# Graph message passing on one core: picked-source sums get PSUM columns of their own, bases are read ahead of a wait, transposed x and the front of the result move in five pieces

## The chip, the cores and the metric

The kernel runs on one core of a Trainium2 chip. The metric is device time in microseconds (us) of one execution. The engines are TensorE (PE, matmuls; PEld, its weight loads), VectorE (DVE), ScalarE (ACT), GpSimd (POOL, which here issues the gathers) and SyncE (SP, which issues most other DMAs). Each engine works through its own instruction list in order and waits on semaphores.

## The reference

Nodes: 12,500 with 48 features. Edges: 400,000, sorted by destination, with 32 features each.

```python
h = jnp.maximum(_layernorm(x, axis=-1), 0.0)
x_i = h[dst]; x_j = h[src]
tmp = jnp.concatenate([x_i, x_j, edge_attr], axis=1)      # 400000 x 128
msg = jax.nn.relu(tmp @ W1 + b1) @ W2 + b2
out = x + jax.ops.segment_sum(msg, dst, num_segments=12500)
```

## The kernel before, in words

**Stage one** (up to about 80 us) normalises the nodes and makes two tables in DRAM, `a_table` (the h rows times the destination part of W1) and `b_table` (times the source part, with b1). It stores them in pieces; the last pieces set when the second stage may begin.

**Stage two** takes the edges in 782 groups of 512. A cycle is nine groups: eight **fetched** groups (696 in all), whose source rows POOL gathers from `b_table` with four indirect DMAs of 128 rows each (`gather_group`, L406), and one **picked** group (86 in all), whose source rows TensorE selects out of an SBUF table of h with one-hot matmuls, with no gather. There are 87 cycles; the last has no picked group of its own. Everything in a cycle is written as eight steps j = 0 to 7, and each engine has its own list of them. For step j, k = 8c + j:

- TensorE: `make_sums(k-3)` (L948, needs `r_ready`, the ReLU of group k-3), `make_z(k-1)` (L940, needs the transposed one-hot of DVE), `run_p(j)` (L964, ten matmuls of the picking), and at even j `fold` of the finished pair through W2 (L954, L955).
- DVE: `add_z(k-3)` (L715, PSUM result plus gathered rows), a share of the picked group's work (`key_hot` L739, `sum_picked` L761 to L769), the one-hots `make_hot` and `make_hot_t` (L695, L707) of group k, then at even j `copy_sums` (L719) and at odd j `add_out` (L730), which adds a folded pair into the result `out_sb` in SBUF at an address read from `base_i` (L729).
- ACT: `take_idx` (L487, gives POOL the indices of group k once the sums of group k-4 are done), `weigh_b2`, `rectify` (L503, the ReLU) and `pick` (L513, scales picked blocks).
- POOL: the gathers of group k, as soon as `idx_ready` allows it; there are four slots of gathered rows.
- SP: the edge, destination and `a_table` loads of group k, as soon as the product of group k-4 is done.

The picked group of cycle c-1 ends in cycle c. Its sums (`make_sums_p`) and its fold (`fold_p`) use the same PSUM columns as the pairs: `ps_sum[:, 0:WIN]`, `ps_out[:, 0:WIN]`, and the same SBUF tile `sums`. Therefore step 7 is written differently from the other odd steps (L1000 and L812 ff.): before anything of group k, DVE does `add_out(k-4)` and `copy_sums_p`, and TensorE does `make_sums_p`, `run_p` and `fold_p`, so that the columns are free in time:

```python
early = j == 7 and not first
if early:
    add_out(k - 4, it)
    copy_sums_p(c - 1, it)
```

**The result** `out_sb` lies in SBUF, transposed (48 x 12,500). It is first filled with transposed x by one DMA (L482) on ACT's queue, issued when both tables are stored, which is just when the second stage starts; the first `add_out` waits for it. At the end, the front 95% of it is stored by one DMA on SP's queue (L344), after SP has issued all loads and when the results that can still change it are in; the rest is stored at the very end (L368).

**The key row** of the first picked group is loaded (L300) after all stores of the tables have been issued.

Of the kernel before, what the change touches and what calls it, by code (L numbers as in the profile page):

```python
# [13 lines left out]
P = 128  # L14
# [13 lines left out]
def gnn(nc, x_main, x_last, x_t, src_t, src_p, dst_t, dst_n, edge_t, w1, b1, w2, b2, out_t):  # L28
# [26 lines left out]
    front = n_nodes * 95 // 100  # L55
    gen_cols, gen_k = 500, 5
# [6 lines left out]
    assert rounds * gen_cols * gen_k == n_nodes  # L63
# [8 lines left out]
    with ctx:  # L72
# [17 lines left out]
        sums = sb("sums", [P, 2 * WIN])  # L90
        idx = sb("idx", [P, SLOTS, TILES], I32)
# [77 lines left out]
        ps_out = ps[0:feat, 3, 0:2 * WIN]  # L169
        ps_cov = ps[0:1, 4, 0:1]  # L170
# [64 lines left out]
        def _(sp):  # L235
# [30 lines left out]

            for c in range(chunks):
# [28 lines left out]
            def load_key(c, it, first=False):  # L296
                n = c + it
                if not first:
                    sp.wait_ge(p_hot_ready, TILES * n)
                sp.dma_start(p_key, key_flat[:, ds(n * e_cols, e_cols)].partition_broadcast(P)).then_inc(p_key_in, 16)  # L300
# [23 lines left out]
            sp.wait_ge(key_stored, 16)  # L324
            sp.wait_ge(h_ready, chunks)
            load_key(0, 0, True)
# [11 lines left out]

            sp.wait_ge(settled_ready, 1)
            front_settled = sp.value_load(settled[0:1, 0:1], min_val=0, max_val=1)  # L340
            with sp.If(front_settled > 0):
                sp.wait_ge(out_added, fetched - late)
                sp.wait_ge(p_out_added, items - 1)
                sp.dma_start(out_t[:, 0:front], out_sb[:, 0:front]).then_inc(out_stored, 16)  # L344
            with sp.Else():
                sp.nop()
# [21 lines left out]
            sp.dma_start(out_t[:, front:n_nodes], out_sb[:, front:n_nodes]).then_inc(out_stored, 16)  # L368
            with sp.If(front_settled < 1):
                sp.dma_start(out_t[:, 0:front], out_sb[:, 0:front]).then_inc(out_stored, 16)  # L370
            with sp.Else():
                sp.nop()
            sp.wait_ge(out_stored, 32)
# [55 lines left out]
        def _(act):  # L429
# [52 lines left out]
            act.dma_start(out_sb, x_t).then_inc(xt_in, 16)  # L482
# [50 lines left out]
            def cycle(c, it, first=False, final=False):  # L533
                for j in range(PERIOD):
# [36 lines left out]
        def _(dve):  # L571
# [149 lines left out]
            def add_out(k, it, after_p=None):  # L721
                dve.wait_ge(folded, it * (PERIOD // 2) + k // 2 + 1)
                if after_p is not None:
                    dve.wait_ge(p_out_added, after_p + it + 1)
                for h in range(2):
                    s, g = it * PERIOD + k - 1 + h, group_of(k - 1 + h, it)
                    if k > 1 or h:
                        dve.wait_ge(out_added, s)
                    base = dve.value_load(base_i[0:1, ds(g, 1)], min_val=0, max_val=n_nodes - WIN)  # L729
                    nc.vector.tensor_tensor(out_sb[:, ds(base, WIN)], ps_out[:, h * WIN:(h + 1) * WIN],  # L730
                                            out_sb[:, ds(base, WIN)], ALU.add).then_inc(out_added, 1)
# [60 lines left out]
            def copy_sums_p(c, it):  # L792
                dve.wait_ge(p_summed, c + it + 1)
                nc.vector.tensor_copy(sums[:, 0:WIN], ps_sum[:, 0:WIN]).then_inc(p_copied, 1)

            def add_out_p(c, it, k):
                n, g = c + it, p_group(c, it)
                dve.wait_ge(p_folded, n + 1)
# [294 lines left out]
```

## Time and profile before

| what | value |
|---|---|
| median of three runs | 3669.01 us (3666.77, 3669.01, 3681.05) |
| profiled execution | 3678.76 us, span 3676.9 us, 1.9 us outside of the span |
| TensorE busy | 3480.5 us (95%), mean granted clock 0.948 of full |
| POOL busy | 2655.2 us (72%), in 2784 gathers |
| DVE busy | 2592.4 us (71%) |
| ACT busy | 1780.6 us (48%) |
| DMA traffic | 380.40 MB, mean 103 GB/s |

The span runs from the first to the last instruction. The busy time of an engine leaves out register, branch, semaphore and DMA-issuing instructions, so the share of POOL above leaves out the time between two gathers.

### The profile page before, as it was taken

To read this page: it belongs to the slowest core of one execution; us is meant where nothing else is said; L and a number is where in the kernel's file an instruction comes from. 1 tells how busy PE (TensorE), PEld (TensorE's weight loads), DVE (VectorE), ACT (ScalarE), POOL (GpSimd) and SP (SyncE) were. 2 spreads that over 40 slices of the span, in tenths; PEclk is the share of its full clock that TensorE was granted. 3 is DMA by queue.
4 is the path that set the end of the run, shared out by engine and by line. 5 is a ranking of instruction groups with operands and counts; after the bars stand their busy time and mean duration, and the time that the engine had idled before them with its cause. 6 is when DMAs were issued, how large, how long until landed. Compare 5 with 4: busy or idle time off the path is not lost.

```text
span 3676.9 us, 90266 instructions
## 1 busy us (share of the span) xinstructions
PE 3480.5 (95%) x22112; PEld 3043.2 (83%) x22112; DVE 2592.4 (71%) x6238; ACT 1780.6 (48%) x5902; POOL 2655.2 (72%) x2800
## 2 busy tenths in 40 slices
PE   7899999999999999999999999999999999999997
PEld 6788888888888888888888888888888888888887
DVE  6667676767777777767776777777776776777674
ACT  5444444444444445444544454444444444445443
POOL 1677777777777777777777777777777777777775
PEclk9899999999999999999999999999999999999997
DMA  8433333333333333333333333333333333333333
GB/s 270 105 98 100 103 97 96 100 104 96 98 97 106 95 98 98 102 97 99 99 100 98 97 101 103 98 98 98 102 99 98 98 103 98 95 99 104 96 98 94
DMA packets 268638, 380.40 MB, mean 103 GB/s; under 512 B 86052, under 2 KB 149333, under 8 KB 267878
## 3 DMA queue, kind: packets, MB, share of 16 engines
q0 software_dynamic: 89088, 182.63, 19.5%
q1 hardware_dynamic: 179462, 195.11, 17.9%
q10 hardware_dynamic: 64, 2.40, 0.5%
q8 instruction: 8, 0.13, 0.0%
q14 instruction: 16, 0.13, 0.0%
HBM read 362.77 MB, written 17.03 MB: 103 GB/s over the span
## 4 chain that ended last, share of the span: by engine, by line
PE 81%; DVE 6%; DVEq 5%; issue 4%; ACT 2%; DMA 1%; SPq 0%; POOL 0%; ACTq 0%; POOLq 0%
PE ps L964 39%; PE ps L940 17%; PE ps L948 16%; PE ps L954 3%; DVEq L729 3%; DVE p_hot L739 2%; PE ps L981 2%; DVE gath L715 2%; PE ps L955 2%; ACT gath L503 2%; DVEq L800 1%; PE ps L974 1%; PE ps L914 1%; DVE nodes L730 1%; DMA rhs<-a_table 1%
## 5 line engine op out<-in xcount | busy, mean ns | idle before, releaser
L406 POOL DMA_INDIRECT gath<-b_table,idx x2784 | 2651.1, 952 | 999.5 <-issue 900.2
L964 PE MATMUL ps<-h_tab,p_hot 128*128 128x480 f32 x6880 | 1793.6, 410 | 9.5 <-DVE p_hot L739 9.5
L964 PEld LDWEIGHTS ps<-h_tab,p_hot 128*128 128x128 f32 x6880 | 1332.2, 202 | 205.4 <-issue 9.6
L513 ACT ACTIVATE work<-ps,work 128x96 f32<-128x96 f32 x3440 | 869.9, 344 | 636.7 <-PE ps L964 597.7
L503 ACT ACTIVATE gath<-gath 128x512 f32<-128x512 f32 x696 | 439.7, 632 | 1110.2 <-DVE gath L715 1110.1
L948 PEld LDWEIGHTS ps<-onehot,gath 128*128 128x128 f32 x5568 | 711.1, 195 | 218.5 <-ACT gath L503 163.1
L948 PE MATMUL ps<-onehot,gath 128*128 128x48 f32 x5568 | 750.0, 279 | 146.3 <-ACT gath L503 146.3
L940 PE MATMUL ps<-rhs,lhs 96*128 96x128 f32 x5568 | 815.1, 291 | 16.3 <-DVE lhs L707 16.3
L940 PEld LDWEIGHTS ps<-rhs,lhs 96*128 96x128 f32 x5568 | 706.9, 199 | 17.0 <-DVE lhs L707 16.9
L730 DVE TENSOR_TENSOR nodes<-ps,nodes 48x48 f32 x696 | 139.4, 200 | 823.1 <-PE ps L955 486.8
L707 DVE TENSOR_SCALAR_CACHE_REDUCE lhs<-nodes 48x512 f32<-48x512 f32 x696 | 517.9, 744 | 50.1 <-DMA rhs<-a_table 19.7
L739 DVE TENSOR_TENSOR p_hot<-work,ps 128x1280 fp32r<-128x1280 f32 x344 | 508.1, 1477 | 8.2 <-DMA work<-key_row 7.4
L715 DVE TENSOR_TENSOR gath<-ps,gath 128x512 f32<-128x512 f32 x696 | 480.9, 691 | 15.6 <-DMA gath<-b_table,idx 7.3
L695 DVE TENSOR_TENSOR onehot<-ps,dst_rel 128x192 f32<-128x192 f32 x696 | 245.2, 352 | 2.7
L496 ACT ACTIVATE b_deg<-b_bc,deg 48x48 f32<-48x48 f32 x696 | 234.7, 337 | 16.8
L761 DVE TENSOR_TENSOR work<-work 128x480 f32<-128x480 f32 x344 | 223.5, 650 | 0.0
L487 ACT COPY idx<-src_sb 128x4 int32 (+1 forms) x692 | 137.4, 199 | 88.4 <-PE ps L948 64.5
L954 PEld LDWEIGHTS ps<-sums,w_sb 128*48 128x48 f32 x696 | 58.0, 123 | 122.1 <-issue 121.2
L763 DVE TENSOR_TENSOR work<-work 128x192 f32<-128x192 f32 x344 | 126.5, 368 | 11.8
L719 DVE COPY sums<-ps 128x96 f32<-128x96 f32 x348 | 88.0, 253 | 65.8 <-PE ps L948 61.8
L954 PE MATMUL ps<-sums,w_sb 128*48 128x96 f32 x696 | 129.1, 268 | 0.4 <-DVE sums L719 0.3
L955 PE MATMUL ps<-pair_ident,b_deg 112*48 112x96 f32 x696 | 115.7, 247 | 0.0
(88 smaller groups left out, 1416.8 us busy)
## 6 DMA issues: line engine op xcount, KB each, us to landing
nodes<-dst_row SPq DMA_DIRECT2D x782, 96.0 KB
lhs<-in_edge_t SPq DMA_DIRECT2D x696, 64.0 KB
gath<-b_table,idx POOLq DMA_INDIRECT x2784
work<-key_row SPq DMA_DIRECT2D x86, 256.0 KB
rhs<-a_table SPq DMA_DIRECT2D x696, 24.0 KB
work<-in_edge_t SPq DMA_DIRECT2D x172, 32.0 KB
b_table<-nodes SPq DMA_DIRECT2D x7, 512.0 KB, 3.3
a_table<-nodes SPq DMA_DIRECT2D x7, 512.0 KB, 5.2
```

Source lines behind the costliest of these rows:

```text
L406: pool.indirect_dma_start(gath[:, u, t, :], None, b_table, bass.IndirectOffsetOnAxis(ap=idx[:, u, t:t + 1], axis=0)).then_inc(gathered[u], 16)
L496: nc.scalar.activation(b2_deg[r:r + WIN, k // 2 % 2, :], b2_bc[0:WIN, :], ACT.Copy, scale=deg[:, u:u + 1]).then_inc(b2_ready, 1)
L503: nc.scalar.activation(z, z, ACT.Relu).then_inc(r_ready, 1)
L513: m = nc.scalar.activation(p_sel[:, t % 2, RUN_COLS * q + j, :], ps_run[:, r % 2, j * split:(j + 1) * split], ACT.Copy, scale=p_mask[:, RU ...
L695: nc.vector.tensor_tensor(onehot[:, u, :, :], iota_ps.unsqueeze(1).to_broadcast([P, TILES, WIN]), dst_rel[:, ds(g * TILES, TILES)].unsquee ...
L707: nc.vector.tensor_scalar(lhs[0:WIN, u, :], dst_bc[:, u, :], first_node[:, ds(g, 1)], None, ALU.is_equal, ALU.add, accum_out=deg[:, u:u + ...
L715: nc.vector.tensor_tensor(z, ps_z[:, k % 2, :], z, ALU.add).then_inc(z_added, 1)
L739: nc.vector.tensor_tensor(p_hot[:, t % 2, :, :], p_key[:, t * P:(t + 1) * P].unsqueeze(1).to_broadcast([P, BLOCKS, P]), key_iota_ps.unsque ...
L940: mm = nc.tensor.matmul(ps_z[:, k % 2, t * P:(t + 1) * P], lhs[:, u, t * P:(t + 1) * P], rhs[:, u, :], start=True, stop=True)
L948: mm = nc.tensor.matmul(ps_sum[:, k % 2 * WIN:(k % 2 + 1) * WIN], gath[:, u, t, :], onehot[:, u, t, :], start=(t == 0), stop=(t == TILES - 1))
L954: nc.tensor.matmul(ps_out, w2_sb[:], sums[:], start=True, stop=False)
L964: mm = nc.tensor.matmul(ps_run[:, r % 2, :].rearrange("p (j w) -> p j w", j=RUN_COLS), p_hot[:, t % 2, i, :], h_parts[:, first:first + BLO ...
```

## The change

1. The picked group's sums and its fold get columns of their own in the same two PSUM banks (`ps_sum_p`, `ps_out_p`, columns 96 to 144), and an SBUF tile `sums_p`.
2. With that, step 7 has the order of the other odd steps. TensorE does `make_sums_p` at the end of step 7 ahead of `run_p`, and `fold_p` at the end of the next cycle's step 0. DVE does `copy_sums_p` in the next cycle's step 0 and `add_out_p` in its step 1. In step 1 `add_out` waits for `fold_p` too, since it reads the same bank.
3. `add_out` reads both bases from `base_i` ahead of its wait for the fold; before, each was read behind the wait. `add_out_p` reads its base ahead of its wait too.
4. The key row of the first picked group is loaded in stage one, ahead of the last chunk's table stores.
5. Transposed x is loaded in five DMAs of 2500 columns, which ACT issues in step 3 of the first cycle, behind the ReLU of group 0.
6. The front of the result is stored in five DMAs of 2375 columns, which SP issues in steps 3 to 7 of the last cycle between its loads.

```diff
+        ps_sum_p = ps[:, 2, 2 * WIN:3 * WIN]
+        ps_out_p = ps[0:feat, 3, 2 * WIN:3 * WIN]
...
+                if c == 5:
+                    sp.wait_ge(key_stored, 16)
+                    sp.wait_ge(h_ready, chunks)
+                    load_key(0, 0, True)
...
+            def store_front(k):
+                part = slice(k * front_piece, (k + 1) * front_piece)
+                if k == 0:
+                    sp.wait_ge(settled_ready, 1)
+                    sp.wait_ge(out_added, fetched - late)
+                    sp.wait_ge(p_out_added, items - 1)
...
+                    if final and j >= 3:
+                        store_front(j - 3)
...
-            act.dma_start(out_sb, x_t).then_inc(xt_in, 16)
+
+            def load_x(k):
+                act.dma_start(out_sb[:, k * piece:(k + 1) * piece], x_t[:, k * piece:(k + 1) * piece]).then_inc(xt_in, 16)
...
+                    if first and k == 3:
+                        for x in range(pieces):
+                            load_x(x)
...
-            def add_out(k, it, after_p=None):
+            def add_out(k, it, after_p=None, beside_p=None):
+                bases = [dve.value_load(base_i[0:1, ds(group_of(k - 1 + h, it), 1)], min_val=0, max_val=n_nodes - WIN)
+                         for h in range(2)]
                 dve.wait_ge(folded, it * (PERIOD // 2) + k // 2 + 1)
+                if beside_p is not None:
+                    dve.wait_ge(p_folded, beside_p + it + 1)
...
-                    early = j == 7 and not first
-                    if early:
-                        add_out(k - 4, it)
-                        copy_sums_p(c - 1, it)
...
-                    if early:
-                        add_out_p(c - 1, it, k - 4)
...
+                        add_out(k - 4, it, c - 2 if j == 3 and c > 1 else None, c - 2 if j == 1 and c > 1 else None)
+                    if j == 1 and c > 1:
+                        add_out_p(c - 2, it, k - 4)
...
+                    if j == 0 and c > 1:
+                        copy_sums_p(c - 2, it)
...
-                    if j == 7 and not first:
-                        make_sums_p(c - 1, it)
-                        if not final:
-                            run_p(j, c, it)
-                        fold_p(c - 1, it)
...
+                    if j == 7 and not first:
+                        make_sums_p(c - 1, it)
+                    if not final:
                         run_p(j, c, it)
                     if j % 2 == 0 and k >= 4:
                         fold(k - 3, it)
+                    if j == 0 and c > 1:
+                        fold_p(c - 2, it)
```

How the lists move: on TensorE, step 7 of a cycle before (L948 is `make_sums`, L940 `make_z`, L964 `run_p`, L988 `make_sums_p`, L993 and L994 `fold_p`; line numbers of the kernel before).

```order
L988 MATMUL ps<-work 128x48 [waits p_r_ready]
L988 MATMUL ps<-work 128x48 x3
L961 REGISTER_ALU
L964 MATMUL ps<-h_tab,p_hot 128x480 [waits p_picked]
L964 MATMUL ps<-h_tab,p_hot 128x480 x9
L993 MATMUL ps<-sums,w_sb 48x48 [waits p_copied]
L994 MATMUL ps<-ident,p_b_deg 48x48
L948 MATMUL ps<-onehot,gath 128x48 [waits r_ready]
L948 MATMUL ps<-onehot,gath 128x48 x3
...
L940 MATMUL ps<-rhs,lhs 128x128 [waits hott_ready]
L940 MATMUL ps<-rhs,lhs 128x128 x3
```

The same step of the changed kernel (its lines stand 22 lines further down: L970 is `make_sums`, L962 `make_z`, L1010 `make_sums_p`, L986 `run_p`).

```order
L970 MATMUL ps<-onehot,gath 128x48 [waits r_ready]
L970 MATMUL ps<-onehot,gath 128x48 x3
L960 REGISTER_ALU
L962 MATMUL ps<-rhs,lhs 128x128 [waits hott_ready]
L962 MATMUL ps<-rhs,lhs 128x128 x3
L1010 MATMUL ps<-work 128x48 [waits p_r_ready]
L1010 MATMUL ps<-work 128x48 x3
L986 MATMUL ps<-h_tab,p_hot 128x480 [waits p_picked]
L986 MATMUL ps<-h_tab,p_hot 128x480 x9
```

The picked fold has left step 7, and the ten picking matmuls now come last in it. On DVE, step 7 of a cycle before, from the copy of the pair's sums of step 6 on (L729 and L730 are `add_out`, L794 `copy_sums_p`, L715 `add_z`, L739 `key_hot`).

```order
L719 COPY sums<-ps 128x96 [waits summed]
...
L729 REGISTER_ALU [waits out_added,folded]
L729 TENSOR_LOAD base_i
...
L730 TENSOR_TENSOR nodes<-ps,nodes 48x48
L729 REGISTER_ALU [waits out_added]
L729 TENSOR_LOAD base_i
...
L730 TENSOR_TENSOR nodes<-ps,nodes 48x48
L794 COPY sums<-ps 128x48 [waits p_summed]
...
L715 TENSOR_TENSOR gath<-ps,gath 128x512 [waits gathered0]
...
L739 TENSOR_TENSOR p_hot<-work,ps 128x1280 [waits p_run_done]
```

The same place of the changed kernel (L734 is `add_z`, L760 `key_hot`, L714 and L726 the one-hots, L741 and L751 `add_out`).

```order
L738 COPY sums<-ps 128x96 [waits summed]
...
L734 TENSOR_TENSOR gath<-ps,gath 128x512 [waits gathered0]
...
L760 TENSOR_TENSOR p_hot<-work,ps 128x1280 [waits p_run_done]
...
L714 TENSOR_TENSOR onehot<-ps,dst_rel 128x192
...
L726 TENSOR_SCALAR lhs,deg<-nodes 48x512
...
L741 TENSOR_LOAD base_i
...
L741 TENSOR_LOAD base_i
...
L751 ISA [waits out_added,folded]
L751 TENSOR_TENSOR nodes<-ps,nodes 48x48
L751 ISA [waits out_added]
L751 TENSOR_TENSOR nodes<-ps,nodes 48x48
```

The wait for the fold has moved from ahead of `add_z` to the end of the step, and both reads of the bases stand ahead of it.

## Rows read from the trace of the kernel before

**Rows 1.** The waits, longest first: engine, line, waited for, us, times, longest

```profile
DVE nodes L730 <- PE ps L955: 486.8, 168, 4.2
PE ps L948 <- ACT gath L503: 146.3, 88, 8.1
POOL gath L406 <- ACT idx L487: 99.3, 155, 16.1
```

**Rows 2.** Timeline of TensorE, one step 7: start, us, line, tile, [idle <-releaser]

```profile
2016.65 2.45 PE L964 MATMUL ps<-h_tab,p_hot 128*128 128x480 f32 x10
...
2020.39 1.12 PE L940 MATMUL ps<-rhs,lhs 96*128 96x128 f32 x8
2023.12 1.09 PE L948 MATMUL ps<-onehot,gath 128*128 128x48 f32 x8 [1.60 <-ACT gath L503]
2024.04 1.23 PE L940 MATMUL ps<-rhs,lhs 96*128 96x128 f32 x8
2024.93 3.99 PE L964 MATMUL ps<-h_tab,p_hot 128*128 128x480 f32 x10
```

**Rows 3.** The same line a cycle later, and two neighbours in another place

```profile
2063.93 1.09 PE L948 MATMUL ps<-onehot,gath 128*128 128x48 f32 x8 [1.60 <-ACT gath L503]
...
3043.20 1.09 PE L948 MATMUL ps<-onehot,gath 128*128 128x48 f32 x8 [1.60 <-ACT gath L503]
...
3082.45 1.42 PE L948 MATMUL ps<-onehot,gath 128*128 128x48 f32 x8 [1.60 <-ACT gath L503]
```

**Rows 4.** Timeline of DVE ahead of that step's add_z

```profile
2016.65 0.20 DVE L730 TENSOR_TENSOR nodes<-ps,nodes 48x48 f32 x1 [4.17 <-PE ps L955]
2017.68 0.20 DVE L730 TENSOR_TENSOR nodes<-ps,nodes 48x48 f32 x1 [0.83 <-DVE nodes L730]
```

**Rows 5.** Timeline of POOL: first waits, a steady stretch, a pause, the last gather

```profile
83.67 1.10 POOL L406 DMA_INDIRECT gath<-b_table,idx  x1 [78.83 <-issue]
...
119.64 0.95 POOL L406 DMA_INDIRECT gath<-b_table,idx  x1 [16.12 <-ACT idx L487]
...
134.65 0.95 POOL L406 DMA_INDIRECT gath<-b_table,idx  x1 [0.30 <-issue]
...
508.60 0.94 POOL L406 DMA_INDIRECT gath<-b_table,idx  x1 [2.04 <-issue]
...
2021.67 0.95 POOL L406 DMA_INDIRECT gath<-b_table,idx  x1 [0.89 <-ACT idx L487]
...
3654.58 0.94 POOL L406 DMA_INDIRECT gath<-b_table,idx  x1 [0.30 <-issue]
```

**Rows 6.** Busy time by stretch: us, busy us of each engine, clock, DMA share, GB/s

```profile
2000.00:2040.00 40.00, 38.40 (x249) 33.41 (x248) 28.78 (x70) 20.05 (x67) 29.96 (x32) 0.96 0.36 101
```

**Rows 7.** The start of stage two on all engines, and the DMA issues

```profile
85.08 0.40 ACTq L482 DMA_DIRECT2D nodes<-in_x_t  x1
85.87 4.04 SPq L294 DMA_DIRECT2D rhs<-a_table  x4
...
107.93 0.74 DVE L707 TENSOR_SCALAR_CACHE_REDUCE lhs<-nodes 48x512 f32<-48x512 f32 x1 [19.68 <-DMA rhs<-a_table]
...
nodes<-in_x_t ACTq DMA_DIRECT2D x1, 2343.8 KB, 22.1
```

**Rows 8.** DMA queues from 89 to 101 us: packets, MB, share (q10 ACT, q0 POOL)

```profile
q10 hardware_dynamic: 32, 1.60, 102.2%
q0 software_dynamic: 17, 0.07, 4.3%
```

**Rows 9.** The end: SP, then DVE, and the store's issue row

```profile
3638.98 0.33 SPq L344 DMA_DIRECT2D out_t<-nodes  x1
...
3656.61 0.69 DVE L715 TENSOR_TENSOR gath<-ps,gath 128x512 f32<-128x512 f32 x1 [7.33 <-DMA gath<-b_table,idx]
...
3667.85 0.67 DVE L715 TENSOR_TENSOR gath<-ps,gath 128x512 f32<-128x512 f32 x1
...
out_t<-nodes SPq DMA_DIRECT2D x1, 2226.6 KB, 17.4
```

More of the change, by code:

```diff
@@ L55, in gnn @@
     front = n_nodes * 95 // 100
+    pieces = 5
+    piece, front_piece = n_nodes // pieces, front // pieces
     gen_cols, gen_k = 500, 5
@@ L62, in gnn @@
     assert PERIOD == 2 * SLOTS
-    assert rounds * gen_cols * gen_k == n_nodes
+    assert rounds * gen_cols * gen_k == n_nodes and piece * pieces == n_nodes and front_piece * pieces == front
     a_table = nc.dram_tensor("a_table", [padded, hidden], F32).ap()
@@ L294, in load_a @@
                 sp.dma_start(rhs[0:WIN, u, :], a_table[ds(base, WIN), :]).then_inc(loaded[u], 16)
[L296 to L300, printed above, removed]
+            def store_front(k):
[4 more added lines that the diff above has]
+                    sp.wait_ge(p_out_added, items - 1)
+                front_settled = sp.value_load(settled[0:1, 0:1], min_val=0, max_val=1)
+                with sp.If(front_settled > 0):
+                    sp.dma_start(out_t[:, part], out_sb[:, part]).then_inc(out_stored, 16)
+                with sp.Else():
+                    sp.nop()
             def load_p(c, it, first=False):
@@ L337, in _ @@
             cycle(cycles - 1, 0, final=True, more=False)
[L339 to L346, printed above, removed]
             sp.wait_ge(flag_ready, 1)
@@ L368, in _ @@
             sp.dma_start(out_t[:, front:n_nodes], out_sb[:, front:n_nodes]).then_inc(out_stored, 16)
+            front_settled = sp.value_load(settled[0:1, 0:1], min_val=0, max_val=1)
             with sp.If(front_settled < 1):
-                sp.dma_start(out_t[:, 0:front], out_sb[:, 0:front]).then_inc(out_stored, 16)
+                for k in range(pieces):
+                    part = slice(k * front_piece, (k + 1) * front_piece)
+                    sp.dma_start(out_t[:, part], out_sb[:, part]).then_inc(out_stored, 16)
             with sp.Else():
                 sp.nop()
-            sp.wait_ge(out_stored, 32)
+            sp.wait_ge(out_stored, 16 * (pieces + 1))
         @block.gpsimd
@@ L725, in add_out @@
                 for h in range(2):
-                    s, g = it * PERIOD + k - 1 + h, group_of(k - 1 + h, it)
                     if k > 1 or h:
[L728 to L731, printed above, removed]
+                        dve.wait_ge(out_added, it * PERIOD + k - 1 + h)
+                    nc.vector.tensor_tensor(out_sb[:, ds(bases[h], WIN)], ps_out[:, h * WIN:(h + 1) * WIN],
+                                            out_sb[:, ds(bases[h], WIN)], ALU.add).then_inc(out_added, 1)
             def key_hot(t, c, it):
@@ L854, in _ @@
                 if k % 2:
-                    add_out(k - 4, 0, items - 1)
+                    add_out(k - 4, 0, None, items - 1)
+                    add_out_p(items - 1, 0, k - 4)
                 else:
                     copy_sums(k - 3, 0)
-            add_out(fetched - 1, 0)
+                if k == fetched:
+                    copy_sums_p(items - 1, 0)
+            add_out(fetched - 1, 0, items - 1)
             outside = dve.value_load(flag[0:1, 0:1], min_val=0, max_val=n_edges)
@@ L1012, in cycle @@
                         make_z_p(c - 1, it)
-                    if not final and (j != 7 or first):
+                    if j == 7 and not first:
+                        make_sums_p(c - 1, it)
+                    if not final:
                         run_p(j, c, it)
@@ L1022, in _ @@
             cycle(0, 0, first=True)
-            with pe.Fori(0, cycles - 2) as it:
-                cycle(1, it)
+            cycle(1, 0)
+            with pe.Fori(0, cycles - 3) as it:
+                cycle(2, it)
             cycle(cycles - 1, 0, final=True)
@@ L1031, in _ @@
                     fold(k - 3, 0)
+                if k == fetched:
+                    fold_p(items - 1, 0)
             outside = pe.value_load(flag[0:1, 0:1], min_val=0, max_val=n_edges)
```

26 lines of the change are left out of this document (14 added, 12 removed).

## The prediction

> **What bounds the kernel now.** I read the waits first. TensorE waits for one thing that counts, the ReLU of the fetched group: 88 times, 146.3 us in all [rows 1]. The timeline of TensorE shows where: once a cycle, in step 7, the second `make_sums` is late [rows 2]. It starts 2.73 us after the `make_z` ahead of it (2020.39 to 2023.12), where the next such pair, which waits for nothing, is 0.89 apart (2024.04 to 2024.93): a stall of 1.84 us. Behind the stall the ten picking matmuls take 3.99 us instead of 2.45: the clock has been taken to its lower level (1.2 GHz) for a while, and that costs 1.54 us more. The same line comes back after 40.81 us (2023.12 to 2063.93) [rows 2, 3], which is the cycle's length. The reader is to check this on the cycle that begins at 3043.20: it took 39.25 us [rows 3], 1.56 less, which is what a cycle costs when the clock does not fall. So TensorE's own work is 40.81 - 1.84 - 1.54 = 37.43 us a cycle.
>
> The cause of the stall is on DVE: `add_out` waits 4.17 us for the fold of step 6, and the `add_z` of step 7 is queued behind it [rows 4].
>
> Then I ask who is next. POOL is 72% busy by its row, but that row leaves out the time between gathers. In the timeline a gather takes 0.95 us and 0.30 passes before the next [rows 5], so 32 gathers of a cycle need 40.0 us at the least. POOL is nearly as full as TensorE. From the gather at 119.64 to the last at 3654.58 there are 2767 steps in 3534.94 us, 86.5 cycles. The waits for ACT's indices are 99.3 us, 155 times [rows 1]; less the first, 16.1, and less 154 usual gaps of 0.30, true waiting is 37.0 us. All the rest is POOL's own, pauses such as the 2.04 us at 508.60 too [rows 5]: 3534.94 - 37.0 = 3497.9 us, **40.44 us a cycle**. TensorE holds the kernel at 40.81, and POOL is 0.37 behind it. DVE is busy 28.8 of 40 us, ACT 20.1 [rows 6].
>
> The start and the end have chains of their own. DVE waits 19.68 us for `a_table` rows that SP issued from 85.87 on, since ACT had issued transposed x at 85.08, which takes 22.1 us to land [rows 7]. From 89 to 101 us that load moves 1.60 MB and fills the engines (102%), while all gathers together get 0.07 MB through [rows 8]. At the end the store of the front does the same: issued at 3638.98, 17.4 us, and `add_z` waits until 3656.61 for gathered rows [rows 9].
>
> **The change, part by part.**
>
> *Step 7.* The stall of 1.84 and, with it, the slow matmuls of 1.54 go: `add_z` is no longer queued behind a wait for the fold, and what `make_sums_p` and `fold_p` do is moved, not added. TensorE's share would be 3.38 x 86.5 = 292 us. But POOL allows only 40.81 - 40.44, that is the 37.0 us of index waits. So the term is **37 us**. Its bounds: at the top POOL also loses its pauses, 3534.94 - 2767 x 1.25 = 76 us; at the bottom a third of the waits turn out to be pauses that are put down to ACT, 25 us.
>
> *The moved pieces.* `fold_p` now lengthens step 0 of TensorE and `copy_sums_p` and `add_out_p` lengthen steps 0 and 1 of DVE, each by well under a microsecond. They lie beside POOL's 40.44: TensorE has 3.0 us a cycle to spare. Without that cover they would cost nothing either, for their number is the same as before. What is late next is the gathered row: TensorE will wait for the ReLU before most steps, some 0.4 us each, as each group's gathers take 40.44 / 8 = 5.05 us and an average step 4.68. The indices of a group are due four groups ahead, so POOL should not feel it.
>
> *The bases.* Between the two adds lie 0.83 us, nearly all of it the read of a base [rows 4]. Read ahead, it hides in the wait for the fold. DVE wins about 0.6 us on each of 348 pairs, and none of it is on the path in the loop: zero. At the very end it is on the path once, 0.8 us, counted below.
>
> *The key row.* Its DVE wait at the start ended long before the 19.68 us one, and rows of a table land last in either order. Zero, or a microsecond either way, as it stands ahead of the last table stores.
>
> *Transposed x.* The `a_table` rows, issued at 85.87, should land at about 88.3 instead of 107.9, and the steps 0 to 3 run about 19.6 us earlier. ACT then issues x near 97. Its bytes still need 15 to 22 us of the same DMA engines, so it lands between 113 and 120 and holds up the gathers of groups 2 to 5 meanwhile. POOL issues these without a pause, as their indices are ready: the 16.12 us gap [rows 5] closes. It next has to stop at group 7, whose indices need the sums of group 3, whose rows land after x: 120, then some 4 us for add, ReLU, sums and indices, so 124.5, against 134.65 before [rows 5]. The term is **10 us**. Bounds: 83.67 + 28 x 1.25 = 118.7, no stop at all, 16 us; and 4 us if the loads of SP that share the queues make x land at 126.
>
> On this the Trainium skill's "DMA: Bandwidth & Descriptors", section "Queues, rings and completion order", says that each DMA engine takes turns between its queues, a packet at a time. The trace agrees, 1.60 MB of long rows against 0.07 MB of gathers [rows 8]. By that rule five shorter pieces let five times as many small packets pass, and the term would be nearer its upper bound, 16 us. I stay with 10: a group's 512 gathered rows are 32 for each of 16 engines, and the 5 x 48 long rows of x give each engine only 15 turns to pass them.
>
> *The front's store.* SP is three to four groups ahead when it issues in steps 3 to 7, so the last piece is out no later than the single store was (3638.98), and needs 17.4 / 5 = 3.5 us: landed by 3645, with POOL gathering until 3655.5. The last rows then land some 2.5 us after POOL ends, and from the last `add_z` at 3667.85 to the end are 9.05 us [rows 9], less 0.8 for the base. The end after POOL's last gather is 10.8 us in place of 3676.9 - 3655.5 = 21.4: **10.6 us**. Bounds 5 (the groups queue up on a TensorE at the lower clock) and 12.
>
> *Sum.* 37 + 10 + 10.6 = 57.6 us. The profiled execution took 3678.8, so its successor would take 3621. It stands 9.8 us above the median of the runs, 3669.0, so the forecast for the median is **3612 us**. With the bounds: 104 us to 34 us, 3565 to 3635.
>
> **The rivals.**
>
> *The whole stall comes back.* If POOL could follow, 292 + 21 us would go: 3356 us. Against it: 1.25 us a gather, 16 times in a row without any wait. 3%.
>
> *POOL's pauses shrink too.* They are not bound to anything that I can name; if they go, 3669 - 76 - 21 = 3572 us. 12%.
>
> *Another wait takes its place.* If the cycle stays at 40.81, for instance since a DVE step of 5.2 us (step 1 has both adds and the picked one) pushes its successors, only start and end are won: 3648 us. For it: four slots couple all engines. Against: DVE's busy share. 12%.
>
> *The clock falls more often: slower.* TensorE now idles once a cycle for 1.84 us and its clock falls once. Afterwards it idles a little before most steps. Each fall costs 1.54 us. POOL's 40.44 covers (40.44 - 37.43) / 1.54 = 2.0 falls a cycle. Start and end give 20.6 us, and 18.3 more makes 0.5%, so the kernel is slower from a cycle of 40.81 + 38.9 / 86.5 = 41.26 on, 2.5 falls a cycle. At three, the cycle is 42.05 and the time 3669 + 107 - 21 = 3755 us. Against it: a TensorE that is behind POOL has no idle time, and then its clock has no reason to fall. 5%.
>
> The Trainium skill's "TensorE: Matmul & The Clock Gate", section "A second HAM failure mode: psum-queue depth-cycling", says that frequent very short idle times between groups of matmuls can make the clock go down and up again. The trace has no such pattern, only one long idle time a cycle; by that rule this rival would be the likeliest, with 3755 us or more.
>
> *Start or end go wrong by over 20 us* (x starves the gathers for longer than before): about 3650 us with the 37 kept. 2%.
>
> **How the numbers follow.** My forecast has 66%, and its own range is 3580 to 3635 us. To leave out no more than 2 in 10, I reach from POOL's pauses (3572) to the case of an unchanged cycle (3648). Half a per cent, 18 us, is about what a measurement tells from no change: 3651 and up is no gain. Faster: 66 + 12 + 3, and 7 of the 12 for the unchanged cycle, 88%. The same: 5 and 2, 7%. Slower: 5%.
>
> **What would show it.** In the changed profile: POOL's waits for ACT's indices nearly gone behind the start; gathers 1.25 us apart through steps 7 and 0; a cycle near 40.4 us; TensorE waiting for ReLU several times a cycle, shortly, with few or no picking groups of 3.9 us; DVE waiting for gathered rows (7.3 us before, once) in hundreds of places; DVE's first one-hot near 88 us and a long wait there for x or for rows near 110 to 120; the end about 11 us behind the last gather. The forecast is wrong if the cycle is not set by POOL: then look for picking groups of 3.9 us (clock), or for index waits that stay (another ring of waits).

## The result

The changed kernel takes 3608.55 us, median of four runs (3607.37 to 3610.1), against 3667.91 for the kernel before (3666.77 to 3681.05): a ratio of 0.983, 95% interval 0.9807 to 0.9853, or 59.4 us less. The forecast was 3612. The profiled execution of the changed kernel took 3607.57 us with a span of 3605.7. That of before stood about 11 us above its median, so a comparison of the two traces shows 71.2 us, not 59.4.

The page of the changed kernel: the busy rows, the chain that ended last, and POOL's group.

```profile
PE 3405.7 (94%) x22112; PEld 2959.7 (82%) x22112; DVE 2592.8 (72%) x6238; ACT 1755.9 (49%) x5902; POOL 2663.1 (74%) x2800
...
PE 46%; POOL 24%; issue 16%; DMA 9%; ACT 3%; DVE 2%; POOLq 0%; ACTq 0%; DVEq 0%
...
L420 POOL DMA_INDIRECT gath<-b_table,idx x2784 | 2659.0, 955 | 929.9 <-issue 887.7
```

The busy rows hardly tell a bound: TensorE still reads 94% and POOL 74%. The chain tells more. POOL, the time between its instructions ("issue") and its transfers (DMA) hold half of it. In the chain of before, PE alone had 81%, and POOL stood at 0%.

The waits of the changed kernel (engine, line, released by: us in total, times, longest):

```profile
POOL gath L420 <- issue: 887.7, 2654, 79.1
DVE gath L734 <- DMA gath<-b_table,idx: 645.4, 588, 8.9
...
PE ps L970 <- ACT gath L519: 169.8, 268, 7.0
...
POOL gath L420 <- ACT idx L503: 42.2, 130, 1.8
...
DVE nodes L751 <- PE ps L977: 37.0, 39, 1.2
```

Read them against [rows 1]. POOL waited for indices 99.3 us, 155 times; now it is 42.2 in 130 times, of which 130 usual gaps of 0.30 are 39, so almost nothing is left. DVE waits for gathered rows 588 times, where it did once. TensorE's wait for the ReLU has grown from 88 times to 268. In the kernel before it was one wait of 1.60 us a cycle; now it is several a cycle, mostly short ones (half of the 268 are under 0.36 us, 69 are over 1 us): the sign of an engine that has caught up with another.

TensorE's timeline over one cycle, the rows that answer to [rows 2] (start, us, instructions, and in brackets the idle time before them):

```profile
2006.07 1.09 PE L970 MATMUL ps<-onehot,gath 128*128 128x48 f32 x8 [0.80 <-ACT gath L519]
...
2020.14 0.25 PE L1015 MATMUL ps<-sums_p,w_sb 128*48 128x48 f32 x2
...
2025.12 1.09 PE L970 MATMUL ps<-onehot,gath 128*128 128x48 f32 x8 [0.33 <-ACT gath L519]
...
2030.10 1.09 PE L970 MATMUL ps<-onehot,gath 128*128 128x48 f32 x8 [0.28 <-ACT gath L519]
...
2035.27 1.09 PE L970 MATMUL ps<-onehot,gath 128*128 128x48 f32 x8 [0.46 <-ACT gath L519]
...
2037.08 2.45 PE L986 MATMUL ps<-h_tab,p_hot 128*128 128x480 f32 x10
...
2040.22 1.09 PE L970 MATMUL ps<-onehot,gath 128*128 128x48 f32 x8 [0.23 <-ACT gath L519]
```

In this cycle no long idle time stands before `make_sums` any more. In its place are short ones of 0.23 to 0.80 us before five of its eight `make_sums` (the row at 2020.14 is `fold_p`, now in step 0), and the last of these come about 5 us apart (2025.12, 2030.10, 2035.27, 2040.22), which is POOL's step of four gathers. The picking groups take 2.45 us here. Over the whole trace, 36 of the 688 picking groups take more than 3.1 us, where 78 of 688 did before, and the mean granted clock rose from 0.948 to 0.975. Such a slow group looks like this:

```profile
1038.69 1.17 PE L970 MATMUL ps<-onehot,gath 128*128 128x48 f32 x8 [1.63 <-ACT gath L519]
...
1041.35 3.17 PE L986 MATMUL ps<-h_tab,p_hot 128*128 128x480 f32 x10
```

Each of the 36 is the first picking group behind an idle time of TensorE of 1.08 us or more; none follows one of the short idle times. Idle times over 1 us are still there (68 behind the start, against 88 before), so the clock fell less often, but such idle times are not gone.

The start of the changed kernel: SP's first loads, DVE's first step, ACT's issues of transposed x, DVE's next wait, and POOL where it has to stop (answers to [rows 5, 7]).

```profile
85.40 4.07 SPq L309 DMA_DIRECT2D rhs<-a_table  x4
...
87.18 0.74 DVE L726 TENSOR_SCALAR_CACHE_REDUCE lhs<-nodes 48x512 f32<-48x512 f32 x1 [6.06 <-DMA rhs<-a_table]
...
94.48 0.40 ACTq L498 DMA_DIRECT2D nodes<-in_x_t  x1
95.86 1.19 ACTq L498 DMA_DIRECT2D nodes<-in_x_t  x2
...
111.25 0.69 DVE L734 TENSOR_TENSOR gath<-ps,gath 128x512 f32<-128x512 f32 x1 [8.91 <-DMA gath<-b_table,idx]
...
115.61 0.94 POOL L420 DMA_INDIRECT gath<-b_table,idx  x1 [1.83 <-ACT idx L503]
...
121.67 0.94 POOL L420 DMA_INDIRECT gath<-b_table,idx  x1 [1.38 <-ACT idx L503]
```

DVE waits 6.06 us for `a_table` rows, not 19.68, and POOL's gap of 16.12 us has become two stops, of 1.83 and 1.38 us. Group 7's first gather starts at 121.67 instead of 134.65.

The DMA queues from 95 to 107 us, when the pieces of x are under way (packets, MB, share of the 16 engines):

```profile
q10 hardware_dynamic: 220, 1.72, 81.9%
q0 software_dynamic: 88, 0.20, 9.3%
q1 hardware_dynamic: 140, 0.18, 9.2%
```

Against [rows 8] the gathers (q0) get 0.20 MB through beside 1.72 MB of x, instead of 0.07 beside 1.60.

The end, answers to [rows 9]: first and last piece of the front, POOL's last gather, DVE's last wait for rows and last adds, and the last store.

```profile
3560.31 0.33 SPq L319 DMA_DIRECT2D out_t<-nodes  x1
...
3576.27 0.33 SPq L319 DMA_DIRECT2D out_t<-nodes  x1
...
3592.80 0.94 POOL L420 DMA_INDIRECT gath<-b_table,idx  x1 [0.30 <-issue]
...
3597.22 0.69 DVE L734 TENSOR_TENSOR gath<-ps,gath 128x512 f32<-128x512 f32 x1 [1.39 <-DMA gath<-b_table,idx]
...
3602.08 0.54 DVE L751 TENSOR_TENSOR nodes<-ps,nodes 48x48 f32 x2 [1.21 <-PE ps L977]
...
3602.80 0.33 SPq L379 DMA_DIRECT2D out_t<-nodes  x1
```

The last wait for rows is 1.39 us (7.33 before). The last two adds take 0.54 us together, with no read of a base between them. And from the start of the last gather to the end of the span are 3605.7 - 3592.8 = 12.9 us, where it was 3676.9 - 3654.6 = 22.3.

**Where the 71.2 us of the traces are.** Group 7's first gather is 13.0 us earlier. From there to the last gather are 2755 steps from gather to gather: 3519.93 us before, 3471.13 now, 48.8 less. The end behind the last gather is 9.4 shorter. 13.0 + 48.8 + 9.4 = 71.2.

### The profile page after: what moved, and what is told of

It is laid out like the page before. It is cut to its first block, busy times and chain, and to the rows that moved or that the text cites. A ratio compares the mean times of both kernels' runs of the same rounds, so it can differ in the third digit from the quotient of the medians.

```text
span 3605.7 us, 90357 instructions
## 1 busy us (share of the span) xinstructions
PE 3405.7 (94%) x22112; PEld 2959.7 (82%) x22112; DVE 2592.8 (72%) x6238; ACT 1755.9 (49%) x5902; POOL 2663.1 (74%) x2800
## 4 chain that ended last, share of the span: by engine, by line
PE 46%; POOL 24%; issue 16%; DMA 9%; ACT 3%; DVE 2%; POOLq 0%; ACTq 0%; DVEq 0%
POOL gath L420 24%; PE ps L986 21%; PE ps L970 10%; PE ps L962 9%; DMA gath<-b_table,idx 9%; PE ps L1010 2%; DVE gath L734 2%; PE ps L976 1%; ACT gath L519 1%; PE ps L936 1%; PE ps L977 1%; ACT work L529 1%; PE ps L996 0%; PE ps L1016 0%; ACT idx L503 0%
## 5 line engine op out<-in xcount | busy, mean ns | idle before, releaser
L420 POOL DMA_INDIRECT gath<-b_table,idx x2784 | 2659.0, 955 | 929.9 <-issue 887.7
L986 PE MATMUL ps<-h_tab,p_hot 128*128 128x480 f32 x6880 | 1725.4, 398 | 2.4 <-DVE p_hot L760 2.4
L986 PEld LDWEIGHTS ps<-h_tab,p_hot 128*128 128x128 f32 x6880 | 1280.4, 194 | 185.1 <-issue 2.4
L970 PEld LDWEIGHTS ps<-onehot,gath 128*128 128x128 f32 x5568 | 693.3, 193 | 312.3 <-ACT gath L519 279.1
L734 DVE TENSOR_TENSOR gath<-ps,gath 128x512 f32<-128x512 f32 x696 | 481.4, 692 | 651.0 <-DMA gath<-b_table,idx 645.4
L970 PE MATMUL ps<-onehot,gath 128*128 128x48 f32 x5568 | 754.5, 279 | 173.9 <-ACT gath L519 169.8
L962 PE MATMUL ps<-rhs,lhs 96*128 96x128 f32 x5568 | 803.0, 289 | 3.3 <-DVE lhs L726 3.3
L962 PEld LDWEIGHTS ps<-rhs,lhs 96*128 96x128 f32 x5568 | 696.9, 196 | 3.8 <-DVE lhs L726 3.7
L726 DVE TENSOR_SCALAR_CACHE_REDUCE lhs<-nodes 48x512 f32<-48x512 f32 x696 | 517.8, 744 | 37.0 <-DMA rhs<-a_table 6.3
L760 DVE TENSOR_TENSOR p_hot<-work,ps 128x1280 fp32r<-128x1280 f32 x344 | 508.2, 1477 | 1.4 <-PE ps L986 1.1
L714 DVE TENSOR_TENSOR onehot<-ps,dst_rel 128x192 f32<-128x192 f32 x696 | 244.9, 352 | 2.7
L751 DVE TENSOR_TENSOR nodes<-ps,nodes 48x48 f32 x696 | 139.2, 200 | 104.9 <-PE ps L977 37.0
L976 PEld LDWEIGHTS ps<-sums,w_sb 128*48 128x48 f32 x696 | 57.6, 122 | 118.1 <-issue 117.4
```

The source lines that it names most:

```text
L420: pool.indirect_dma_start(gath[:, u, t, :], None, b_table, bass.IndirectOffsetOnAxis(ap=idx[:, u, t:t + 1], axis=0)).then_inc(gathered[u], 16)
L714: nc.vector.tensor_tensor(onehot[:, u, :, :], iota_ps.unsqueeze(1).to_broadcast([P, TILES, WIN]), dst_rel[:, ds(g * TILES, TILES)].unsquee ...
L726: nc.vector.tensor_scalar(lhs[0:WIN, u, :], dst_bc[:, u, :], first_node[:, ds(g, 1)], None, ALU.is_equal, ALU.add, accum_out=deg[:, u:u + ...
L734: nc.vector.tensor_tensor(z, ps_z[:, k % 2, :], z, ALU.add).then_inc(z_added, 1)
L760: nc.vector.tensor_tensor(p_hot[:, t % 2, :, :], p_key[:, t * P:(t + 1) * P].unsqueeze(1).to_broadcast([P, BLOCKS, P]), key_iota_ps.unsque ...
L962: mm = nc.tensor.matmul(ps_z[:, k % 2, t * P:(t + 1) * P], lhs[:, u, t * P:(t + 1) * P], rhs[:, u, :], start=True, stop=True)
```

## The experiments

Each kernel ran beside the kernel before on the same chip. Six runs stand apart: where they ran, the kernel before took about 5210 us instead of 3668. They are told at the end.

**1. Step 7 alone.** The kernel before, with the picked sums' own columns, the moved pieces of step 7 and the early bases. Transposed x, the key row and the front's store stay as they were, so that what their new places could win is taken out:

```diff
 kernel before, plus:
+        sums_p = sb("sums_p", [P, WIN])
+        ps_sum_p = ps[:, 2, 2 * WIN:3 * WIN]
+        ps_out_p = ps[0:feat, 3, 2 * WIN:3 * WIN]
...
-                    early = j == 7 and not first
```

> The same kernel as in the first group of runs, which met a chip on which even the kernel before took 5213 us, all engines standing still for some us at a time. Theory, where the kernel before takes its 3668 us: only the steady part is won, 37 us (25 to 56), so 3631 us (3612 to 3643), with POOL's 16 us gap at group 4 and the 21 us end still there. Rival (the gain lies in the start and the end): no more than 5 us won.

Measured: 3630.89 us against 3666.70, ratio 0.9906 (0.9889 to 0.9922), 35.8 us less. The trace's waits:

```profile
POOL gath L411 <- issue: 892.4, 2666, 79.8
DVE gath L721 <- DMA gath<-b_table,idx: 657.1, 597, 16.9
...
PE ps L957 <- ACT gath L509: 176.0, 274, 13.7
```

TensorE waits 274 times and DVE 597 times for rows, as in the changed kernel. POOL's waits for indices beyond the usual gap are 5.8 us behind group 7, one single stop (6.12 us, the gather at 3607.13) that the front's store brings about, as experiment 5 shows. So the forecast's term of 37 us holds, with 35.8, and it comes from the edits of step 7 and the bases, without start and end. The trace parts it otherwise: from group 7 on, its gathers need 3475.77 us instead of 3519.93, 44.2 less.

**2. The ends alone.** The changed kernel with step 7 and the adds as before:

```diff
 changed kernel, minus:
-        sums_p = sb("sums_p", [P, WIN])
...
+                    early = j == 7 and not first
+                    if early:
+                        add_out(k - 4, it)
+                        copy_sums_p(c - 1, it)
```

> The kernel before with x in five late pieces, the early key row and the front in five pieces; step 7 as before, again. Theory: start 13 and end 9 us as in the changed kernel's trace, so 22 us won, 3646 us, and a cycle of 40.8 us as before. With the 36 us of the step-7 edits alone that makes 58, the 59 of the whole change. Rival (a start won earlier is given back in the loop): under 10 us won.

Measured: 3653.64 us against 3672.10, ratio 0.9954 (0.9939 to 0.9969), 18.5 us less. 22 us were expected; what came is 3.5 less, within the interval. The cycle is as before, and so are the two waits that make it:

```profile
DVE nodes L746 <- PE ps L971: 486.5, 169, 4.2
...
PE ps L964 <- ACT gath L516: 146.3, 89, 8.0
```

The end in this trace, POOL's last gather and DVE's last `add_z`:

```profile
3641.91 0.94 POOL L417 DMA_INDIRECT gath<-b_table,idx  x1 [0.30 <-issue]
...
3649.61 0.67 DVE L731 TENSOR_TENSOR gath<-ps,gath 128x512 f32<-128x512 f32 x1
```

The start wins 9.9 us (group 7's first gather at 124.77 instead of 134.65), but the end only 5.5: from the last gather to the end of the span (3658.7) are 16.8 us, where the changed kernel has 12.9. The last `add_z` waits for no rows and still starts 7.7 us behind the last gather, 4.4 in the changed kernel. I read this so that part of the shorter end comes only together with the new step 7, when TensorE and DVE are no longer behind POOL; no run tests it by itself.

The two halves add up roughly: 35.8 + 18.5 = 54.3 us, of the whole change's 59.4. The remaining 5 are within the intervals; the stop of 5.8 us that step 7 alone meets, and this end, are two places where the halves help each other.

**3. Less work for TensorE.** If POOL sets the cycle, a shorter TensorE wins little. Two of the ten picking matmuls of each group are left out. The kernel then leaves out two blocks of the source table, so picked rows from them are missing:

```diff
-                for i in range(BLOCKS):
+                for i in range(BLOCKS - 2):
```

> The changed kernel with 8 instead of 10 picking matmuls a step (two blocks of the picked group's sources are left out), again, where the kernel before takes its 3668 us. TensorE has some 3.9 us a cycle less work. Theory (POOL's gathers set the cycle): no change, within 8 us of the changed kernel's 3608. Rival (TensorE still sets it): some 3 us x 86 = 260 us faster.

Measured: 3594.26 us against 3666.70, ratio 0.9802 (0.9786 to 0.9819), 72.4 us less than before and so 13 less than the change itself. Two tenths of 2.45 us, eight times, are 3.9 us of matmuls a cycle, 340 us in all, and the time gives back 13. That is more than the 8 us that the expectation allowed, and far from its rival's 260. TensorE's waits, and POOL's group:

```profile
PE ps L970 <- ACT gath L519: 371.6, 409, 10.3
```
```profile
L420 POOL DMA_INDIRECT gath<-b_table,idx x2784 | 2645.1, 950 | 932.5 <-issue 883.0
```

TensorE waits 371.6 us where it waited 169.8, some 200 of the 340. Nearly all of the rest went into slower matmuls: the mean granted clock is 0.954 instead of 0.975, and TensorE's busy time fell by 212 us only (3193.5 against 3405.7). It idles over 1 us 123 times behind the start, not 68, and 72 of the 688 picking groups, not 36, are over a quarter longer than usual. And the 13 us are on POOL's side: the mean gather is 950 ns instead of 955, 2784 x 5 ns = 14 us.

**4. Less work for POOL.** The opposite test: three gathers in a group instead of four. The fourth tile's gathered rows are left out (they read as zero), so the result lacks them.

```diff
-                for t in range(TILES):
+                for t in range(TILES - 1):
```

> The changed kernel with three instead of four gathers a group, again (the fourth tile's rows are left out and stay zero or what they were), where the kernel before takes its 3668 us. POOL then needs 30 us a cycle. Theory: TensorE takes over at its own 37.4 us a cycle, 2.9 us less than the 40.3 of the changed kernel, 86.5 times: 250 us less, about 3360. Rival (another ring of waits stands just behind, DVE for instance): a cycle of 39 us or more, 3500 or above.

Measured: 3330.06 us against 3672.10, ratio 0.9070 (0.9055 to 0.9086). Waits, chain, and two picking groups a cycle apart:

```profile
POOL gath L422 <- ACT idx L505: 741.8, 586, 11.0
```
```profile
PE 97%; DMA 1%; DVE 1%; issue 0%; ACT 0%; SPq 0%; DVEq 0%; ACTq 0%; POOL 0%; POOLq 0%
```
```profile
1999.91 2.43 PE L989 MATMUL ps<-h_tab,p_hot 128*128 128x480 f32 x10
...
2036.98 2.43 PE L989 MATMUL ps<-h_tab,p_hot 128*128 128x480 f32 x10
```

Now POOL waits, 586 times, and the chain is 97% PE. The cycle is 2036.98 - 1999.91 = 37.07 us with no idle time on TensorE within it: this is TensorE's own need, which the forecast put at 37.43 from a stall and a slow group taken off. The difference, 0.36 us in 86.5 cycles, is the 30 us by which the time came out below the expected 3360. Together, 3 and 4 show which engine sets the pace of the changed kernel: POOL, with 40.3 us a cycle, some 3 us above TensorE's need. They take gathers away whole; whether POOL's own work or its queue makes the 1.25 us of a gather, they do not tell.

**5. The front in one store.** The changed kernel, with the front stored in one piece behind all of SP's loads, as before:

```diff
-                    if final and j >= 3:
-                        store_front(j - 3)
...
+                sp.dma_start(out_t[:, 0:front], out_sb[:, 0:front]).then_inc(out_stored, 16)
```

> The changed kernel with the front stored by one DMA after all loads, as before. Theory (the long rows of that store hold the last gathers up): 9 us slower than the changed kernel, 3617, and DVE waits some 7 us for gathered rows near the end. Rival (the end is short because of the new step order and the early bases): within 2 us of 3608.

Measured: 3619.96 us against 3672.10, ratio 0.9863 (0.9846 to 0.9879). That is 52.1 us less than before instead of 59.4 (the kernel before took 4 us more on this chip), so the pieces are worth 7 to 11 us; the forecast had 9.8 for them, beside 0.8 for the last base. The one store, DVE's wait behind it, and POOL's stop:

```profile
3574.45 0.33 SPq L350 DMA_DIRECT2D out_t<-nodes  x1
```
```profile
3591.77 0.69 DVE L726 TENSOR_TENSOR gath<-ps,gath 128x512 f32<-128x512 f32 x1 [17.31 <-DMA gath<-b_table,idx]
```
```profile
3596.13 0.94 POOL L412 DMA_INDIRECT gath<-b_table,idx  x1 [6.27 <-ACT idx L495]
```

Issued at 3574.45, it holds gathered rows back: DVE waits 17.31 us for them, where some 7 were expected, and that reaches POOL four groups on, as a stop of 6.27. From the last gather (3599.88) to the end (3618.1) are 18.2 us, not 12.9. So the single store costs at two places: 6.0 on POOL and 5.3 behind it. (The other 1 us or so of the 12.4 between the two spans comes from the start, 2.6 us later here, and from gathers that otherwise need 1.5 less.)

**6. Transposed x in one piece, at the new place.**

```diff
-                        for x in range(pieces):
-                            load_x(x)
+                        load_x()
```

> The changed kernel with x in one DMA at the new, late place. Theory (what counts is the place, behind the rows of a_table; the bytes hold the gathers up for 15 to 20 us either way): within 4 us of the changed kernel, 3608 to 3612. Rival (by the turns of the queues, long rows let fewer gathers pass): gathers of groups 2 and 3 wait some 6 us longer, POOL stops for longer at group 6, 3614 or more.

Measured: 3617.46 us (3610.74 to 3618.99) against 3672.10, ratio 0.9855 (0.9839 to 0.9872), 54.6 us less than before and 5 to 9 us short of the changed kernel. The expectation allowed 4, so this is its rival's outcome (3614 or more, with a longer stop of POOL at group 6). The profiled execution was the fastest of the four, 3610.74. The trace says where the time went: POOL's stop, DVE's wait for rows, and the queues from 95 to 107 us.

```profile
122.36 1.33 POOL L420 DMA_INDIRECT gath<-b_table,idx  x1 [8.02 <-ACT idx L503]
...
128.70 0.94 POOL L420 DMA_INDIRECT gath<-b_table,idx  x1 [1.26 <-ACT idx L503]
```
```profile
118.00 0.69 DVE L733 TENSOR_TENSOR gath<-ps,gath 128x512 f32<-128x512 f32 x1 [15.13 <-DMA gath<-b_table,idx]
```
```profile
q10 hardware_dynamic: 32, 1.60, 96.2%
q0 software_dynamic: 33, 0.07, 2.4%
```

In one piece, x lets 0.07 MB of gathers through in these 12 us; in five it lets 0.20 MB through, nearly three times as much, and group 7 starts at 121.67 instead of 128.70. So of the 13.0 us of the start, 6.0 are due to the new place and 7.0 to the pieces, by these two traces. The traces of experiments 2, 3 and 5 have the same five pieces, and there group 7 starts at 124.77, 124.19 and 124.29. Part of that spread lies ahead of it: POOL's first gather starts at 83.97 in the changed kernel, 84.53 here, and 85.09 to 85.95 in those three (83.67 before). From the first gather to group 7 are 51.0 us before, 44.2 with one late piece and 37.7 to 39.7 with five. So the place is worth some 6 to 7 us and the pieces 4 to 7.

**7. The runs at 5210 us.** In these six runs, engines stood still for several us at a time, in every kernel, with no releaser that the profile knows ("remote" in the rows below). Kernels 1 to 4 ran under these conditions first and then again as told above. Their first runs took 4901.42 us (step 7 alone, ratio 0.9407), 5176.50 (ends alone, 0.9933), 4871.75 (eight picking matmuls, 0.9349) and 3877.15 (three gathers, 0.743), against 5212.65. What they were expected to do:

> The kernel before with the step 7, PSUM and base edits alone; x, the key row and the front's store stay as before. Theory (POOL sets the cycle once the stall is gone): only the steady part is won, 37 us (25 to 56), so 3631 us (3612 to 3643), with POOL's 16 us gap at group 4 and the 21 us end still there. Rival (the gain lies in the start and the end, the cycle stays 40.8): no more than 5 us won, 3663 or more.

> The kernel before with x in five late pieces, the early key row and the front in five pieces; step 7 as before. Theory: start 13 and end 9 us as in the changed kernel's trace, so 22 us won, 3646 us, a cycle of 40.8 us as before. Rival (TensorE, not POOL, is late in a cycle, so that a start won earlier is given back): under 10 us won.

> The changed kernel with 8 instead of 10 picking matmuls a step (two blocks of the picked group's sources are left out), so TensorE has some 3.9 us a cycle less work. Theory (POOL's gathers set the cycle): no change, within 8 us of the changed kernel's 3608. Rival (TensorE still sets it, with short waits and clock falls): some 3 us x 86 = 260 us faster.

> The changed kernel with three instead of four gathers a group (the fourth tile's rows are left out and stay what they were). POOL then needs 30 us a cycle. Theory: TensorE takes over at its own 37.4 us a cycle, 2.9 us less than the 40.3 of the changed kernel, 86.5 times: 250 us less, about 3360. Rival (another ring of waits stands just behind, DVE for instance): a cycle of 39 us or more, 3500 or above.

Two more were meant to place what was left: where TensorE takes over, with two more picking matmuls that add nothing to the sums, and what the early bases bring, with their reads behind the wait again.

```diff
+                for e in range(2):
+                    nc.tensor.matmul(
+                        ps_run[:, r % 2, :].rearrange("p (j w) -> p j w", j=RUN_COLS), p_hot[:, t % 2, e, :],
+                        h_parts[:, e:e + BLOCKS * (RUN_COLS - 1) + 1:BLOCKS, :], start=True, stop=True)
```

> The changed kernel with two picking matmuls more per group that add nothing to the sums (TensorE gets about 3.9 us more work per cycle of eight groups; its own need was about 37.4 us, so about 41.3). Theory (POOL's 40.3 us per cycle sets the pace, TensorE has about 3 us to spare): the first 3 us of the 3.9 are free and only 0.9 us or so per cycle shows, 86.5 cycles x 0.9 = 80 us over the changed kernel, near 3690 us; POOL's waits for an index come back. Rival (TensorE still sets the pace in the changed kernel): 86.5 x 3.9 = 340 us more, near 3945. Rival (TensorE has more to spare than its busy rows say): within 20 us of the changed kernel.

```diff
-                bases = [dve.value_load(base_i[0:1, ds(group_of(k - 1 + h, it), 1)], min_val=0, max_val=n_nodes - WIN)
-                         for h in range(2)]
...
+                    base = dve.value_load(base_i[0:1, ds(group_of(k - 1 + h, it), 1)], min_val=0, max_val=n_nodes - WIN)
```

> The changed kernel with the two reads of the node bases back behind the wait for the picked sums. Theory (VectorE is off the path): nothing that can be told, 3609 us within 5. Rival (the reads ahead of the wait shorten VectorE's part of the step, which TensorE waits for): up to 0.6 us on 348 pairs of steps with a share of it on the path, some 50 us or more slower, near 3660.

They took 4876.71 us (0.9365, 0.9341 to 0.9389) and 4890.56 us (0.9402, 0.9378 to 0.9426) against 5209.91. The waits of the kernel with twelve:

```profile
ACT work L529 <- remote: 1843.8, 274, 9.2
POOL gath L420 <- ACT idx L503: 1278.1, 390, 5.2
```

Here POOL waits 1278.1 us for indices, where it waits 42.2 in the changed kernel's own trace, so neither question is answered: the bound there is another. All that can be read is that eight or twelve picking matmuls make no difference there (4871.75 and 4876.71 us), and that both halves of the change keep their sign. How many us more per cycle TensorE can take on an undisturbed chip, and whether the early bases bring anything, stay open.

## Why the prediction was right, step by step

- **Step 7, 37 us.** Right in mechanism, and in size by the medians: 35.8 us by itself (experiment 1). The one long stall a cycle goes, and POOL takes the pace over. The two traces show 48.8 us for the same stretch. The index waits that the sum counted are 36.5 of it, as forecast. But the profiled execution of before also had pauses that the sum counted as POOL's own: 21 of more than 0.4 us behind group 7, 19.7 us beyond the usual gap. In the changed kernel there is none. 13.1 us of that come back as gathers that take longer (151 of them over 0.97 us, 30.0 us in all above the usual, against 128 and 16.9), and some 2 ns less per step make the other 5.7. The gathers of the whole kernel became 7.9 us longer (2659.0 against 2651.1).
- **How much of the hit is luck.** The sum was made for the traces, 57.6 us, and they show 71.2. The median was then put 9.8 us under the profiled execution, as before the change; but the profiled execution of the changed kernel stands 1 us under its median. The two misses cancel nearly, and 59.4 by the medians is what is left. Whether the other executions of before had fewer pauses is not known, as only one was traced.
- **POOL's own need, 40.44 us a cycle.** It came out as 3471.13 / 2755 x 32 = 40.32. The sentence that pauses "are not bound to anything that I can name" was the weak one. They keep to a count of gathers and go when the index waits go: see the last section.
- **TensorE's need, 37.43 us.** 37.07 when POOL is relieved (experiment 4). Cover for the moved pieces was 3 us, and no run shows that they cost anything; the early bases and the key row were not shown apart.
- **The start, 10 us.** It brought 13.0 in the changed kernel's trace, and 9.9, 10.5 and 10.4 in the three others with the same start. Group 7 was put at 124.5 and starts between 121.67 and 124.77. So the size holds, and it lies at the lower end of what was measured.
- The rule of the Trainium skill's "DMA: Bandwidth & Descriptors", section "Queues, rings and completion order", is that an engine takes turns between its queues by the packet. The traces agree: 220 packets of x let 88 packets of gathers and 140 of q1 pass, and 32 long ones 33 of gathers. That pieces help was right by it; the term of 16 us that the prediction worked out from it was too high, and "five times as many small packets" were 2.7 times.
- **The end, 10.6 us.** 9.4 by the traces (12.9 us behind the last gather instead of 22.3). What it missed is that a single store also stops POOL when it comes early (experiment 5), and that with step 7 as before the pieces win 5.5 only (experiment 2), near the lower bound that the prediction gave for groups that queue up on TensorE.
- **Rivals.** "The whole stall comes back" fails on POOL: 13 us for 340 us of matmuls. "Another wait takes its place" fails: 40.3 us a cycle. "The clock falls more often" fails here: 36 slow groups instead of 78, clock 0.975 instead of 0.948. "POOL's pauses shrink too" came in part: all pauses went, and longer gathers took 7.9 us of the 19.7 back.
- By the rule of the Trainium skill's "TensorE: Matmul & The Clock Gate", section "A second HAM failure mode: psum-queue depth-cycling", slower by the clock was the likeliest. The idle times of 0.2 to 0.8 us did not bring it about here: in the changed kernel each slow group stands behind an idle time of at least 1.08 us. The direction of the rule shows in experiment 3: more idle times over 1 us (123 against 68), more slow groups (72 against 36), a clock of 0.954. So this rival was closer than the argument "has no idle time" made it: TensorE behind POOL does idle, in 268 places.

## What to carry to other kernels

The busy share of an engine that issues transfers leaves out the time between its instructions: here a POOL of 72% needed 40.44 of the 40.81 us of a cycle. Read start to start in the timeline before you price a stall on another engine, since the next bound, not the stall, sets the gain (292 us of stall and slow matmuls, 36 us of gain). A long transfer beside small ones is worth moving behind the first steps, and worth cutting into pieces as well: here each brought some 4 to 7 us of the start.

## What the runs showed of the hardware

- POOL's longest pauses are tied to the number of gathers. In the kernel with only the ends changed, two of them:

```profile
501.14 0.94 POOL L417 DMA_INDIRECT gath<-b_table,idx  x1 [2.04 <-issue]
...
633.38 0.94 POOL L417 DMA_INDIRECT gath<-b_table,idx  x1 [1.86 <-issue]
```

These are the second gathers of groups 80 and 106, so 26 groups or 104 gathers apart, and groups 184, 210, 288, 314 and on to 626 follow on the same comb, though not every 26th group has one. In the kernel before the one at 508.60 [rows 5] is at group 80 too, the next at 106, 184, 288, 314. With three gathers a group, two of them are

```profile
752.11 0.94 POOL L422 DMA_INDIRECT gath<-b_table,idx  x1 [1.20 <-issue]
...
915.18 0.94 POOL L422 DMA_INDIRECT gath<-b_table,idx  x1 [1.27 <-issue]
```

at groups 142 and 177, which is 35 groups or 105 gathers. So something that turns over after some 104 gathers stops POOL. What it is, no run shows; and in the changed kernel and in experiments 1, 3, 5 and 6, where POOL waits for an index beyond the usual gap behind group 7 once at most, no pause over 0.4 us is left on the comb or elsewhere. Why it needs a POOL that also waits is open, and nothing was tried on it.
- A gather of POOL is not of one length: 0.94 us mostly, up to 1.42 in the changed kernel. The long ones of the changed kernel (67 over 1.1 us) all but one fall on the third or fourth gather of step 0 or on the fourth of step 4, and with fewer matmuls in the step there are 30. But in the kernel before, with all ten matmuls, there are 31, so the number of matmuls alone does not decide it; the cause is open.
- One piece of 2343.8 KB, 32 packets of it in 12 us, took 96% of the DMA engines' time and left 2.4% to 33 packets of gathers (experiment 6).
- Slow picking groups stood behind TensorE's longer idle times only. In the kernel before and in those of experiments 1, 2, 3, 5 and 6, every slow picking group is the first one behind an idle time of TensorE of 1.02 us or more. The changed kernel has 185 idle times of 0.2 to 1 us behind the start, and no slow group follows one of them. Not every longer one brings a slow group: 33 of the 68 over 1 us did. In a slow group of before, from 2025 to 2029, the granted clock was 0.58.
